# Packing the weights of an expert into one transfer of 128 long rows

## What is computed

```python
x = x + _L0_xattn_ref(_layernorm(x), ..., ctx_2048, ctx_2048, wq, wk, wv, wo)
x = x + _L0_ffn_ref(_layernorm(x), L0_ffn_w_gate, wi_0, wi_1, wo)          # 8 experts, top 2, width 256
x = x + _L1_xattn_ref(_layernorm(x), ctx_2048, mask_BxS2_bk0)
x = x + _L1_ffn_ref(_layernorm(x), gate_w, w_gate, w_up, w_down)           # 32 experts, top 8, width 192
```

```python
routing_weights = softmax(xt @ gate_w.T); top_w, top_idx = top_k(routing_weights, 8)
g = silu(einsum('th,ehi->eti', xt, w_gate)); u = einsum('th,ehi->eti', xt, w_up)
y = einsum('eti,eih->eth', g * u, w_down)
out = einsum('eth,te->th', y, full_w)       # full_w: the chosen weights, normalised, else zero
```

## Time and profile before

| | us |
|---|---|
| median of 3 runs | 1074.34 |
| lowest and highest | 1072.41, 1076.64 |
| the profiled execution | 1074.04 |
| its span, first to last instruction | 1072.3 |
| the first expert layer, about | 300 to 425 |
| the second expert layer, about | 610 to 1045 |

### The profile page before, as it was taken

One profiled execution on the slowest core, in us unless ns is written; L12 is line 12 of the kernel. 1 busy time (PEld: TensorE's weight loads), 2 busy tenths in 40 slices (PEclk: granted clock), 3 DMA queues, 4 the chain that ended last, 5 costly groups with the idle time before them and its releaser, 6 DMA issues.

```text
span 1072.3 us, 20533 instructions
## 1 busy us (share of the span) xinstructions
PE 800.4 (75%) x5262; PEld 438.2 (41%) x5263; DVE 517.3 (48%) x1531; ACT 517.8 (48%) x764; POOL 476.3 (44%) x397
## 2 busy tenths in 40 slices
PE   3999999999538995477984177777777778777770
PEld 2555455555324442233542043444444444444440
DVE  6344345555444552556884244544544535453432
ACT  2334234445436663135563065566656556655550
POOL 3420000001235774300777555666766566656560
PEclk9999999999769998697996599999999999999995
DMA  8501100000147876901111358878997878779668
GB/s 278 177 20 60 60 31 22 29 31 31 31 130 206 210 174 104 321 2 50 47 47 33 94 134 217 217 156 203 220 233 195 227 168 197 182 186 230 150 111 255
DMA packets 106088, 146.55 MB, mean 137 GB/s; under 512 B 18080, under 2 KB 59296, under 8 KB 106048
## 3 DMA queue, kind: packets, MB, share of 16 engines
q0 software_dynamic: 25760, 56.56, 26.6%
q1 hardware_dynamic: 77696, 89.30, 25.6%
q10 hardware_dynamic: 2592, 0.19, 0.2%
HBM read 103.15 MB, written 42.86 MB: 136 GB/s over the span
## 4 chain that ended last, share of the span: by engine, by line
PE 38%; DMA 18%; issue 11%; DVE 11%; DVEq 8%; ACT 5%; SPq 4%; POOL 3%; ACTq 2%; POOLq 0%
PE pst L181 31%; DMA big<-in_L_ffn_w_down_dram 8%; DMA x_rows<-mid,small 6%; DVEq L1100 3%; DMA mid<-moe_normalised_rows,small 3%; DVEq L1094 2%; PE pst L1204 2%; PE pst L453 2%; POOL moe_tokens_of_experts L934 2%; DMA big<-x_rows 1%; DVE big L1086 1%; DVE xn L284 1%; ACT big L1068 1%; DVE stats L272 1%; PE pst L893 1%
## 5 line engine op out<-in xcount | busy, mean ns | idle before, releaser
L181 PE MATMUL pst<-big,mid 128*128 (+1 forms) x1392 | 278.1, 351 | 28.7 <-DVE mid L1315 16.6
L934 POOL DMA_INDIRECT moe_tokens_of_experts<-token_no,small x80 | 83.7, 1046 | 307.0 <-DVE small L987 286.9
L1398 POOL DMA_INDIRECT x_rows<-mid,small x100 | 161.1, 1611 | 130.2 <-ACT mid L1259 66.4
L181 PEld LDWEIGHTS pst<-big,mid 128*128 128x128 f16 x1392 | 134.6, 100 | 137.7 <-issue 43.8
L1388 POOL DMA_INDIRECT mid<-moe_normalised_rows,small x106 | 113.9, 1075 | 90.3 <-DVE small L1305 29.3
L1204 PE MATMUL pst<-big,mid 128*128 x520 | 129.8, 382 | 1.4 <-ACT mid L1251 0.9
L1240 ACT ACTIVATE mid<-pst 128x1024 f16<-128x1024 f16 x102 | 103.8, 1017 | 54.2 <-PE pst L1176 47.2
L1176 PE MATMUL pst<-id,mid 128*128 128x128 f16 x816 | 64.8, 224 | 59.6 <-DMA mid<-moe_normalised_rows,small 54.2
L1315 DVE SCALAR_TENSOR_TENSOR mid<-pst,small,mid 128x192 f32<-128x192 f32 (+1 forms) x100 | 42.6, 426 | 118.4 <-ACT mid L1246 117.6
L181 PE MATMUL pst<-ctxN,mid 128*128 128x512 f16 x384 | 89.8, 392 | 3.2 <-ACT mid L577 3.2
L1176 PEld LDWEIGHTS pst<-id,mid 128*128 128x128 f16 x816 | 51.6, 100 | 94.4 <-DMA mid<-moe_normalised_rows,small 40.4
(11 more groups left out here) (197 smaller groups left out, 1163.0 us busy)
## 6 DMA issues: line engine op xcount, KB each, us to landing
big<-in_L_ffn_w_gate_dram SPq DMA_DIRECT2D x32, 384.0 KB
big<-in_L_ffn_w_up_dram SPq DMA_DIRECT2D x32, 384.0 KB
big<-in_L_ffn_wi_dram SPq DMA_DIRECT2D x16, 512.0 KB
big<-in_L_ffn_w_down_dram SPq DMA_DIRECT2D x32, 256.0 KB
big<-in_L_ffn_w_down_dram SPq DMA_DIRECT2D x64, 128.0 KB
moe_normalised_rows<-xn SPq DMA_DIRECT2D x18, 256.0 KB, 2.0
mid<-in_ctx_dram SPq DMA_DIRECT2D x16, 256.0 KB, 5.1
x_rows<-big SPq DMA_DIRECT2D x16, 256.0 KB, 8.0
```

Source lines behind the costliest of these rows:

```text
L181: last = nc.tensor.matmul(dst, stationary(a, c), moving(b, c), start=(k == 0), stop=(k == 3 * len(parts) - 1))
L934: nc.gpsimd.indirect_dma_start(out=self.tab_d[:, :], out_offset=bass.IndirectOffsetOnAxis(ap=self.addr[j % 2][:, k:k + 1], axis=0), in_=to ...
L1398: nc.gpsimd.indirect_dma_start(out=acc_d[p][:, :], out_offset=bass.IndirectOffsetOnAxis(ap=self.si[p], axis=0), in_=self.y[p], in_offset=N ...
```

## The change

The host lays out the weights of an expert as 128 rows: row p holds rows p, 128+p, 256+p and 384+p of gate and of up side by side, then row p of down, then the row of down that its second buffer holds at p, with the last 64 rows twice where they are paired. In the second layer a row is 2560 floats (10 KB), in the first 3072 floats (12 KB). The raw buffers become one (`raw`), with `gur` and `dr` as views of it at the places that they had, and a load is one transfer. The bytes moved stay the same. The counts of the waits for loads follow. Apart from that, the 14 routing semaphores are made once and shared by both layers, the second waiting for counts that are 8 higher (`self.b`, the number of tiles before it).

```diff
-                self.gur = carve(big, 0, 2 * GU, F32, "p (s c i) -> p s c i", s=2, c=ND)
-                o = 4 * GU
-                self.dr = carve(big, o, 4 * D, F32, "p (s c n) -> p s c n", s=2, c=2)
-                o += 8 * D
+                self.raw = carve(big, 0, 2 * W, F32, "p (s w) -> p s w", s=2)
+                self.gur = self.raw[:, :, 0:GU].rearrange("p s (c i) -> p s c i", c=ND)
+                self.dr = self.raw[:, :, GU:W].rearrange("p s (c n) -> p s c n", c=2)
+                o = 4 * W
...
             def norm_low(self, dve, j):
-                dve.wait_ge(self.xhi_s, j + 1)
+                dve.wait_ge(self.xhi_s, self.b + j + 1)
...
             def load(self, sp, e, s):
-                sp.dma_start(self.gur[:, s, :, 0:self.I], self.wg[e, :, :].rearrange("(c p) i -> p c i", p=P)).then_inc(self.w_in, 16)
-                sp.dma_start(self.gur[:, s, :, self.I:], self.wu[e, :, :].rearrange("(c p) i -> p c i", p=P)).then_inc(self.w_in, 16)
-                if self.paired:
-                    R = self.I - P
-                    sp.dma_start(self.dr[:, s, 0, :], self.wd[e, 0:P, :]).then_inc(self.w_in, 16)
-                    sp.dma_start(self.dr[0:R, s, 1, :], self.wd[e, P:self.I, :]).then_inc(self.w_in, 16)
-                    sp.dma_start(self.dr[P - R:P, s, 1, :], self.wd[e, P:self.I, :]).then_inc(self.w_in, 16)
-                else:
-                    sp.dma_start(self.dr[:, s, :, :], self.wd[e, :, :].rearrange("(c p) n -> p c n", p=P)).then_inc(self.w_in, 16)
+                sp.dma_start(self.raw[:, s, :], self.packed[e, :, :]).then_inc(self.w_in, 16)
...
-                        sp.wait_ge(self.w_in, 16 * self.NLD * e)
+                        sp.wait_ge(self.w_in, 16 * e)
...
+def pack(np, gate, up, down):
+    E, D, I = gate.shape
+    gu = np.concatenate([w.reshape(E, D // P, P, 1, I) for w in (gate, up)], 3)
+    gu = gu.transpose(0, 2, 1, 3, 4).reshape(E, P, -1)
+    last = down[:, P:] if I % P == 0 else np.concatenate([down[:, P:], down[:, P:]], 1)
+    return np.concatenate([gu, down[:, :P], last], 2)
```

More of the change, by code:

```diff
@@ L19, with program @@
 KEY = 65536
-def program(nc, x_in, ctx_in, mask_in, wq, wk, wv, wo, g0_in, wi0, wi1, wo0, g1_in, wg1, wu1, wd1, out):
+def program(nc, x_in, ctx_in, mask_in, wq, wk, wv, wo, g0_in, w0_in, g1_in, w1_in, out):
     B, S, D = x_in.shape
@@ L478, in values @@
                 if self.first and i >= 2:
-                    pe.wait_ge(self.next.nt_out, i - 1)
+                    pe.wait_ge(self.next.nt_out, self.next.b + i - 1)
                 if not self.first and i >= 2:
@@ L733, in dve @@
                 self.next.place(dve, NT - 1)
+        route = {n: sem(f"routing_{t}") for n, t in (
+            ("lg_full", "logits_full"),
+            ("top_s", "largest_logit_ready"),
+            ("m_s", "choice_ready"),
+            ("pr_s", "logits_exponentiated"),
+            ("rk_full", "ranks_full"),
+            ("key_s", "keys_ready"),
+            ("addr_s", "table_rows_ready"),
+            ("sw_s", "weight_sum_inverted"),
+            ("w_s", "router_weights_ready"),
+            ("row_s", "row_normalised"),
+            ("xhi_s", "row_high"),
+            ("xlo_s", "row_low"),
+            ("nt_full", "x_transposed"),
+            ("nt_out", "x_transposed_moved"),
+        )}
         class Experts:
@@ L755, in program, with __init__ @@
             ROW = 12
-            def __init__(self, name, wg, wu, wd, router, K, before, group):
+            def __init__(self, name, packed, router, K, before, group, before_tiles):
                 self.group = group
+                self.b = before_tiles
+                self.lg_full = route["lg_full"]
+                self.top_s = route["top_s"]
+                self.m_s = route["m_s"]
+                self.pr_s = route["pr_s"]
+                self.rk_full = route["rk_full"]
+                self.key_s = route["key_s"]
+                self.addr_s = route["addr_s"]
+                self.sw_s = route["sw_s"]
+                self.w_s = route["w_s"]
+                self.row_s = route["row_s"]
+                self.xhi_s = route["xhi_s"]
+                self.xlo_s = route["xlo_s"]
+                self.nt_full = route["nt_full"]
+                self.nt_out = route["nt_out"]
                 self.before = before
-                self.wg, self.wu, self.wd, self.router, self.K = wg, wu, wd, router, K
-                self.E, _, self.I = wg.shape
-                I = self.I
+                self.packed, self.router, self.K = packed, router, K
+                self.E, _, W = packed.shape
+                self.I = I = (W - 2 * D) // (2 * ND)
                 E = self.E
@@ L1556 @@
     for name in _INS:
-        a = _np.ascontiguousarray(inputs[name])
+        if isinstance(name, tuple):
+            a = pack(_np, *(_np.asarray(inputs[n]) for n in name))
+            name = name[-1]
+        else:
+            a = _np.ascontiguousarray(inputs[name])
         arrays[f"in_{name}_dram"] = a
```

78 lines of the change are left out of this document (31 added, 47 removed).

## The result

| | before | after | ratio, 95% interval |
|---|---|---|---|
| median of 14 runs each, us | 1072.46 | 1079.43 | 1.0064 [1.0046, 1.0081] |
| lowest and highest | 1067.75, 1076.64 | 1075.54, 1082.27 | |
| span of the profiled execution | 1072.3 | 1075.9 | |

The kernel became 0.64% slower, where 1% faster was forecast. The time lies above the range of 1052 to 1078.

A forecast was written before the change was run, and what follows sets the result against it. The prediction saw the second expert layer as a loop of waits between engines, no engine being full. Its terms, -10 - 1 - 2 + 3 = -10 us, took the profiled 1074.04 us to 1064, range 1052 to 1078.

The forecast's parts named there:

- Issues: free: SyncE's load issue: five issues become one, which by itself was to bring nothing, as data move from about 1 us on.
- Own work, 4.1 to 3.5 us: Transfer time of one load's own weights on the DMA engines: 3.5 us against 4.0 to 4.2, so 0.6 less.
- The bad end of 4.8 us: Upper end for a load's own transfer, at an instruction fetch's 17 GB/s per engine: 0.7 us more a load.
- Sharing, T = 6 us: Second-layer loads beside queue 0: at most 8 of its packets an engine go between, so a load takes 5.8 to 6.1 us.
- the sign of being wrong from the start: In the profile after: a load's own work not below 4 us, or queue 0 still passing more than 8 packets an engine.
- The four long stalls, -10.0: ScalarE's four long waits for weights in the second expert layer, 17.5 us together: loads landing sooner were to save 10.0 us.
- "Against it", +3: Gathers or scatters meeting a load wait for its turns: 12 of 24 late gathers 0.25 us later on average, 3 us lost.
- The two prices of a turn: Weights' time per queue 0 packet when a gather or scatter meets a load: 0.44 us after, against 0.13 before.
- "In the first expert layer ... 1.6 us of waits": First expert layer: rows of 12 KB replace rows of 1 and 2 KB, counted as costing nothing, with 1.6 us of weight waits.
- The rival "slower": Long weight rows block gathers, 1.2 us for each, and scatters, 2.5 us: 1084 us (1078 to 1094), chance 0.11.
- Scatters, -2: Scatters on the chain beside a load were to end 0.6 us sooner; three such, 2 us saved.
- faster than 1069: Chance that the whole kernel runs below 1069 us, given as 0.61 from the forecast's 0.46 and 0.15.

## Why the prediction was wrong, point by point

**Issues: free.** Right: no kernel with a single issue shows a wait in its place. (The 2.8 us given for the issues stands in no row; they begin over 2.25 us. No term hangs on it.)

**Own work, 4.1 to 3.5 us.** Half right. Queue 1 worked 0.4 us less a load, not 0.6. By the Trainium skill's rule of 512 B (DMA: Bandwidth & Descriptors, Specifications) nothing would have been left to gain; the runs differ from it by that 0.4, of which the 64 small packets of completion that went may be a part. The bad end of 4.8 us, taken from an instruction fetch, didn't occur.

**Sharing, T = 6 us.** Right for three of the four: from issue to split 5.70 us (826.61 to 832.31), 6.29 (839.47 to 845.76) and 6.31 (967.06 to 973.37), for 5.8, 6.0 and 6.1; beside the first two queue 0 passed 118 and 112 packets, 7 an engine. For the first of the four long ones it was 8.7 (645.50 to 654.18), not 6.1. Queue rows of that load, from 645.5 to 654.2 us, and of its last part, 652 to 654.2:

```profile
q0 software_dynamic: 399, 0.97, 48.8%
q1 hardware_dynamic: 144, 1.31, 45.4%
```

```profile
q0 software_dynamic: 192, 0.47, 84.6%
q1 hardware_dynamic: 16, 0.06, 7.4%
```

399 packets of queue 0, 25 an engine, went by, not 8, so the sign of being wrong from the start, more than 8 an engine, was there in this load. From 646.5 to 652 us the sums are alike (128 packets of queue 1, 131 of queue 0), but not the parts: 16 to 44 until 648, 49 to 44 until 650, 63 to 43 until 652. Of the last 16 packets six were rows, the last of them from 652.90 to 653.30, and ten were small ones of completion; 192 of queue 0 went by with them, and the load had landed at 653.80. The sum had taken strict turns of rows. It held for the other three and not here; why the last rows came so late isn't shown.

**The four long stalls, -10.0.** The waits went as forecast: in all, 8.7 us remain where 15 were expected. The steps gave 8.1.

**"Against it", +3: the step that failed.** It gave 12 late gathers 0.25 us each, from a turn of 0.44 us in place of 0.13. A gather that meets a load took 7.21 us where it took 6.20, so 1 us more (0.6 to 1.8 over all kernels with either transfer), and 3 to 4 us more where it met one only after the change. TensorE waited 1.9 to 3.0 us in six steps, which lost 15.6 us, 1.7 to 3.5 each. Behind each of the six waits the clock was lower for a stretch (2 us for the twelve products at 771.00), for which the sum had no term; nor had it one for a load that moves closer to a gather. The two prices of a turn are not borne out either: in the meetings of before some nine packets of weights went by for each packet of queue 0, and now 1.2. What misled me was a mean over late landings. A load is at most 6 of 13.6 us in flight, so on average little happens; but the loop puts one gather 0.95 us ahead of about every fourth load, every time, and in all eight cases TensorE stood waiting for it.

**"In the first expert layer ... 1.6 us of waits": costs nothing.** Wrong, and the larger part in this execution: 4.1 us of 3.6 net. I looked there for what could be won, the waits for weights, and not for what could be lost, the gathers, which met the 12 KB rows twice and held TensorE for 2.55 and 2.78 us.

**The rival "slower".** It named the cause: long rows hold up the gathers. Its price for a gather, 1.2 us, is near what was measured (1.0, and 0.6 to 1.8 over all kernels), though it was worked out from turns, which the counts above don't show. It decides, it said, from 0.34 us of mean delay on 38 late landings, 13 us; the loss in the six steps and the first layer was 15.6 + 5.2. Its 1084 doesn't follow from its own sum: a third of its 32 us is 11, less than the 13 gained, so no loss; 1084 needs 23 us of delay. It had the chance 0.11; the result lies between it and the forecast, at the low end of the 1078 to 1094 that it spanned. The case for it was on the page: each tile has a gather, and nothing excluded that one is always close to the load. The issue times of both, side by side, would have shown this before the change was made (the earlier trace rows has the loads; the gathers' issues were not read).

**Scatters, -2.** Not confirmed: the share of scatters on the chain is 6% before and after.

**The chances.** All of the forecast, 0.48, lies at or below 1069, so "faster than 1069" should have been 0.63 and not 0.61.

What stays open: how an engine chooses between two queues; whether the lower clock or the wait itself is the larger part of each lost step in general; why 2 KB rows delay gathers; and the stage times of single executions differ too much for finer sums (the second layer, unchanged but for semaphores, took 419.4, 412.5 and 416.6 us in the profiles of three kernels), so the split of the loss between the layers rests on the ratios of the kernels that pack one of them, 1.0043 and 1.0035, whose sum is above the 1.0039 of both on that chip.

## What to carry to other kernels

When bulk transfers share the DMA engines with small, urgent ones of another queue, long rows speed up the bulk and hold up an urgent transfer that was issued just ahead of it, and a middle length (here 5 KB, 0.5% faster than before, where 10 KB was 0.4 to 0.6% slower) can win on both sides. Before changing either, put the issue times of both in one table; a fixed small offset in a loop counts for more than the mean load on the queues, and moving one issue by 0.7 us was worth up to 0.8%. And look at what may be lost in each stage, not only at what can be won.

## What the hardware showed that was not expected

- Beside a gather, 101 packets of a load with rows of 10 KB went by for 82 of the gather's queue, but 773 for 81 with rows of 768 B and 2 KB: the share of packets depends on the rows, and is not one to one.
- The last 6 of 128 rows of a load and 10 small packets took from 652.0 to 653.8 us, while 192 packets of another queue went by until 654.2.
- A wait of 2.27 us on TensorE was followed by 5 us with a granted clock of 0.50, and so cost twice its length; behind one of 2.41 us in another kernel the clock stayed at 1.00.
- The landing of a gather that meets a load doesn't grow steadily with the load's row: 5.8 us with 1 KB rows, 6.7 with 2 KB, 6.1 with 2.5 KB, 6.3 and 6.45 with 5 KB, 6.8 to 7.3 with 10 KB. The same transfers differ by up to 0.7 us from one profiled execution to another (5.5 to 6.2 with the five transfers of before).
